# The experts' constants of the second FFN: products on GpSimd in place of most one-column matmuls

## The chip, the cores and the metric

The kernel runs on one core of one Trainium2 chip. The metric is the time of one execution on the device, in microseconds. TensorE multiplies matrices (PE in the rows, PEld its weight loads), VectorE (DVE) and ScalarE (ACT) work on tiles and read TensorE's results, GpSimd (POOL) works on tiles in SBUF alone, and SyncE (SP) issues the transfers.

## The reference, cut to what matters

The network adds four layers to 1024 rows of 256 numbers: an attention and an FFN with two experts, then a second attention and a second FFN with eight experts. The change lies in the second FFN:

```python
for e, (w1, b1, w2, b2) in enumerate(expert_params):
    hm = h * mask[..., e:e + 1]
    acc = acc + (_gelu(_gelu(hm) @ w1 + b1) @ w2 + b2)
out = out + acc * gate[..., k:k + 1]
```

A row that is not the expert's own is masked to zero, and the expert then still gives `_gelu(b1) @ w2 + b2`: a constant vector of 128 numbers for each expert, the same for all rows. The hidden sizes are 128, 256, 384, 512 and the same again, so `w2` of the eight experts has 1, 2, 3, 4, 1, 2, 3 and 4 chunks of 128 rows, 20 in all.

## The kernel before, in words

The rows lie in 8 tiles of 128; the attentions work tile by tile, the FFNs on 4 groups of two tiles. Each layer is cut into small steps, named by layer, tile or group, step and number. `make_orders` is a list scheduler in Python that runs when the program is built: `COST` gives each step's engines and estimated times, `steps_and_needs` what it must wait for, and among the steps that an engine could start next, `URGENCY` (with `SWITCH`, `CHANGE` and `SLACK`) picks one. Each engine then carries out its list strictly in that order, and semaphores see to what it depends on. Tiles of the layers are mixed in this way, so that attention steps fill the waits of the FFN steps.

Steps that the text speaks of:

- First attention, tile t: `ln` writes the normed queries in split form to QS (VectorE); `tq` has SyncE transpose QS into QT by DMA from tile 3 on; `s` scores into a bank S and VectorE's maximum and subtraction (MN, PT); `e` ScalarE's exponential; `p` transposes of PT; `o`, `n` the weighted values and back.
- First FFN, group g: `ln` writes XN; `x` transposes XN into a bank S, and ScalarE copies it to XT; `r` the routing matmuls (WR); `u` a block of up matmuls into a bank H, ScalarE's leaky ReLU to R, GpSimd's square to A; `d` the down matmuls, which read A.
- Second FFN, group 0 only: `b` ScalarE's gelu of the biases, GB1; `z`, four steps of two experts each: 20 fp32 matmuls in all, weights W2 (128x128), moving operand one column of GB1, into banks S, which VectorE negates into Y0n. The last one adds up Cb, which ScalarE reads when it takes the shared expert's result (`y` 0) into ACC; the other experts' results get Y0n as a bias.

In the order before, the four `z` steps stand on TensorE behind the scores of tile 2 and ahead of `x` of the first FFN's group 0. An fp32 matmul shows as two records in the profile. A bank that is to be filled is claimed first: its last reader must be done. All matmuls go through the helper at L1325, so the rows tell them apart by their tiles.

Of the kernel before, what the change touches and what calls it, by code (L numbers as in the profile page):

```python
# [4 lines left out]
fp32 = mybir.dt.float32  # L5
bf16 = mybir.dt.bfloat16
u32 = mybir.dt.uint32
ALU = mybir.AluOpType
ACT = mybir.ActivationFunctionType
AX = mybir.AxisListType  # L10
# [49 lines left out]
def ring_of(s):  # L60

    if (s[0], s[2]) == ("attn0", "s") and s[1] < 2:
# [20 lines left out]
                 e="act .2 dve 1.5", t="act .2 dve 2.0", d="pe .87 act 1.13", g="pe .13 act .36", c="pe .86 act .94",  # L83
                 w="pe .43", y="act .47 dve .88", o="pe 1.3 dve .42", st="sp .5", b="act .22", z="pe 1.12 dve .16")}
COST = {part: {s: [(e, float(d)) for e, d in zip(text.split()[::2], text.split()[1::2])] for s, text in costs.items()}
        for part, costs in COST.items()}
# [8 lines left out]
MODE_CHANGE = 0.09  # L95
SWITCH = 12396.8
CHANGE = 244.4
SLACK = {"act": 0.2, "dve": 0.151, "pe": 0.064, "pool": 0.216, "sp": 0.391}
GELU = {("ffn1", s) for s in "bdc"}
EXP = {("attn0", "e"), ("attn1", "p"), ("ffn0", "g"), ("ffn1", "e"), ("ffn1", "t")}  # L100
URGENCY = {
# [15 lines left out]
}  # L117
# [36 lines left out]
def steps_and_needs():  # L154
# [9 lines left out]
    def need(s, f, part=0, of=-1):  # L164
        needs.setdefault((s, part), []).append((f, of % len(work_of(f))))
# [79 lines left out]
    def ffn1(g):  # L245
        def f(name, i=0, g=g):
            return "ffn1", g, name, i
# [11 lines left out]
        for i, (e, c) in enumerate(WORK):  # L259
            if i % 2 == 0:  # L260
                add(f("c", i // 2), f("d"))
                if i >= 4:
                    need(f("c", i // 2), f("w", min(i + 1, NCH1 - 1) - 4), part=1)
            add(f("w", i), f("c", i // 2))
            if c == CH1[e] - 1 and e == EXPERTS[1]:
                need(f("w", i), f("g"))
            if c == CH1[e] - 1:
                j = EXPERTS.index(e)
                add(f("y", j), f("w", i))
                if j == 0 and g == 0:  # L270
                    need(f("y", j), f("z", E1 // 2 - 1))
        for k in range(2):
            add(f("o", k), f("y", E1))
            add(f("st", k), f("o", k))
        if g == 0:
            add(f("b"))
            for i in range(E1 // 2):
                add(f("z", i), f("b"))
            need(f("t"), ("const", 0, "g", 0))
# [119 lines left out]
def mixed_network(nc: bass.Bass, x, ctx_in, ctxT, wr0, wf0, wp0, wq1, wkv1, wo1, down_w, down_b,  # L399
                  up_w, bias_rows, router_w, router_rows, core_w, w1, b1, w2, b2, out):  # L400
    ctx = ExitStack()
    with ctx:
# [39 lines left out]
        earlier = sb("earlier", [P, E1, E1], fp32)  # L442
        mhalf = sb("mhalf", [P, 2], fp32)
        rbias = sb("rbias", [P, E1], fp32)
        GB1 = sb("GB1", [P, NCH1], fp32)
# [14 lines left out]
        QR = sb("QR", [P, 2, D], fp32)  # L460
        QS = sb("QS", [P, 2, NH0, 64], bf16)
        KR = sb("KR", [P, 2, CTX], fp32)
        KS = sb("KS", [P, 2, NKV0, 4, 64], bf16)
# [180 lines left out]
        biased = sem("biased")  # L644
        zeros_ready = sem("zeros_ready")
        dve_step = sem("dve_step")
        pool_step = sem("pool_step")
# [245 lines left out]
        def _(pool):  # L893
# [61 lines left out]
            def biases(g, _):  # L955
# [5 lines left out]
                for t in (2 * g, 2 * g + 1):  # L961
                    nc.gpsimd.tensor_tensor(X[:, t, :], X[:, t, :], BR[:, 0, :], ALU.add).then_inc(biased, 1)

            def square(g, i):
                n = g * BLOCKS0 + i
# [37 lines left out]
            def gate_rows(*_):  # L1003

                link(nc.gpsimd.memset(flat(selG[:, :, :]), 0.0))
                for part in range(PARTS):
# [9 lines left out]
                         ("ffn0", "v"): norm("ffn0"), ("ffn1", "v"): norm("ffn1"), ("attn1", "kv"): keys1,  # L1016
                         ("ffn1", "i"): biases, ("ffn0", "u"): square})


        @block.vector  # L1020
        def _(dve):
# [235 lines left out]

            def zero_row(g, i):

                b, done = filled(dve, "ffn1", g, "z", i)  # L1260
                nc.vector.tensor_scalar(Y0n[:, 2 * i:2 * i + 2], b[:, 0:2], -1.0, None, ALU.mult).then_inc(done, 1)
                if i == E1 // 2 - 1:

                    total = lsum["ffn1"][:, 0:1]
                    read_out(dve, "ffn1", g, "z", i)
                    dve.wait_ge(ld_small, 16 * SMALL)
                    link(nc.vector.tensor_tensor(Y0s[:, :], B2[:, 0:E1], Y0n[:, :], ALU.subtract))
                    link(nc.vector.tensor_reduce(total, Y0s[:, :], AX.X, ALU.add))
                    nc.vector.scalar_tensor_tensor(Cb[:, :], B2[:, E1:E1 + 1], 0.1, total, ALU.mult, ALU.add
                                                   ).then_inc(zeros_ready, 1)  # L1270

# [33 lines left out]
            def first_queries(t, i):  # L1305
                queries0(t, i)
                if t == 1:
# [9 lines left out]
                 ("ffn1", "v"): variance("ffn1"), ("ffn1", "ln"): rows("ffn1"), ("ffn1", "r"): logits1,  # L1317
                 ("ffn1", "e"): two_largest, ("ffn1", "t"): gates1, ("ffn1", "z"): zero_row,
                 ("ffn1", "y"): expert, ("ffn1", "o"): result_ffn1})
# [3 lines left out]
        def _(pe):  # L1323
# [219 lines left out]

            def zero_row(g, i):
                b, done = claim(pe, "ffn1", g, "z", i)
                if i == 0:
                    pe.wait_ge(ld_w2, 16)
                    pe.wait_ge(gb1_ready, 1)
                for e in (2 * i, 2 * i + 1):
                    for c in range(CH1[e]):  # L1550
                        ch = FIRST1[e] + c
                        ins = mm(b[:, e % 2:e % 2 + 1], W2[:, ch, :], GB1[:, ch:ch + 1], start=(c == 0), stop=(c == CH1[e] - 1))
                ins.then_inc(done, 1)
# [31 lines left out]
            def widen(g, k):  # L1585
# [5 lines left out]
                if k == 0:  # L1591
# [16 lines left out]
                 ("ffn0", "d"): down0, ("ffn1", "x"): turn_rows("ffn1"), ("ffn1", "r"): route("ffn1", XT1, RW, E1),  # L1608
                 ("ffn1", "g"): turn_gates, ("ffn1", "d"): narrow, ("ffn1", "z"): zero_row, ("ffn1", "c"): up1,
                 ("ffn1", "w"): down1, ("ffn1", "o"): widen})  # L1610
# [52 lines left out]
```

## Time and profile before

| | |
|---|---|
| median of 3 runs | 370.07 us (370.01 to 371.87) |
| profiled execution | 374.63 us |
| its span, first to last instruction | 372.8 us |
| TensorE busy | 342.8 us, 92% |
| VectorE, ScalarE, GpSimd busy | 221.9, 179.9 and 96.0 us |
| mean granted clock of TensorE | 0.954 of full speed |

Busy time is read from one execution under the hardware profiler; the median comes from runs of the same program without it. Times in rows count from the span's start.

### The profile page before, as it was taken

The numbers are of one execution on the slowest core, as the hardware profiler recorded it, in microseconds if no ns is written. First come the engines' busy times: TensorE is split into PE (matmuls) and PEld (weight loads), VectorE is DVE, ScalarE is ACT, GpSimd is POOL, SyncE is SP. The second block draws the span as 40 slices with busy tenths as digits, with TensorE's granted clock in tenths as the row PEclk, the third lists the DMA queues.
The fourth block names the chain that finished last, engine by engine and source line by source line (L and its number), as shares of the span: only waits on it lengthen the run. The fifth ranks groups of instructions, "written<-read, shape, count | busy, mean of one in ns | idle before, by whom it ended". The sixth has DMA issues, their size and how long they took to land.

```text
span 372.8 us, 8427 instructions
## 1 busy us (share of the span) xinstructions
PE 342.8 (92%) x3352; PEld 279.6 (75%) x3352; DVE 221.9 (60%) x586; ACT 179.9 (48%) x381; POOL 96.0 (26%) x175
## 2 busy tenths in 40 slices
PE   0677599999999999999999999999999998996996
PEld 0455598887888887878778787888687876784883
DVE  7996976979596825670762265754636483267024
ACT  1656735444542454421222553466586646765462
POOL 7886323332232113134252223310101200020000
PEclk9957958999999999999999999999999999998799
DMA  9999630633603500306300340330042330000000
GB/s 187 417 380 243 133 58 0 114 43 72 114 3 67 102 2 4 58 1 114 57 2 3 35 62 20 59 58 0 22 86 39 58 65 22 2 2 29 0 0 30
DMA packets 62295, 25.75 MB, mean 69 GB/s; under 512 B 58544, under 2 KB 60848, under 8 KB 61488
## 3 DMA queue, kind: packets, MB, share of 16 engines
q1 hardware_dynamic: 62256, 25.21, 30.8%
q8 instruction: 27, 0.44, 0.5%
q14 instruction: 12, 0.10, 0.1%
HBM read 10.52 MB, written 1.05 MB: 31 GB/s over the span
## 4 chain that ended last, share of the span: by engine, by line
PE 81%; DVE 13%; issue 2%; ACT 2%; POOL 1%; DVEq 0%; POOLq 0%
PE Y L1325 27%; PE H L1325 24%; PE S L1325 20%; PE S L1370 5%; PE S L1394 1%; DVE MN L1092 1%; DVE PT L1093 1%; PE S L1403 1%; PE S L1485 1%; DVE K L1079 1%; ACT PT L761 1%; DVE X L1292 1%; DVE K L1302 0%; ACT PT L804 0%; DVE statsf L1041 0%
## 5 line engine op out<-in xcount | busy, mean ns | idle before, releaser
L1325 PE MATMUL H<-XT,WF 128*128 128x256 f32 x256 | 61.5, 388 | 0.0
L1325 PE MATMUL Y<-WP,A 128*128 128x256 f32 x256 | 59.7, 381 | 0.0
L969 POOL TENSOR_TENSOR A<-R 128x512 f32<-128x512 f32 x32 | 33.7, 1056 | 77.2 <-ACT R L837 71.5
L1325 PEld LDWEIGHTS H<-XT,WF 128*128 128x128 f32 x256 | 47.4, 193 | 6.6
L1325 PEld LDWEIGHTS Y<-WP,A 128*128 128x128 f32 x256 | 47.4, 190 | 6.4 <-POOL A L969 0.2
L1325 PE MATMUL Y<-A,W 128*128 128x256 f32 x168 | 46.5, 391 | 0.5 <-DVE KS L1278 0.4
L865 ACT ACTIVATE A<-H,B 128x256 f32<-128x256 f32 x84 | 35.4, 473 | 22.6 <-PE H L1325 22.4
L1325 PE MATMUL H<-CD,W 128*128 128x256 f32 x168 | 44.6, 397 | 0.0
L1278 DVE TENSOR_TENSOR KS<-KS,Y 128x256 f32<-128x256 f32 x32 | 13.4, 420 | 43.2 <-ACT KS L883 42.9
L837 ACT ACTIVATE R<-H 128x512 f32<-128x512 f32 x32 | 19.1, 596 | 37.6 <-PE H L1325 34.2
L1325 PEld LDWEIGHTS H<-CD,W 128*128 128x128 f32 x168 | 32.1, 199 | 5.2
L1325 PEld LDWEIGHTS Y<-A,W 128*128 128x128 f32 x168 | 29.9, 193 | 7.2 <-ACT A L865 1.3
L761 ACT COPY PT<-S 128x512 f32<-128x512 f32 x32 | 18.1, 588 | 21.2 <-PE S L1370 21.2
L804 ACT ACTIVATE PT<-PT 128x512 f32<-128x512 f32 x32 | 19.6, 627 | 9.6 <-DVE PT L1093 9.3
L1370 PE MATMUL S<-identf,PT 128*128 128x128 f32 x128 | 22.1, 320 | 1.0 <-ACT PT L804 1.0
L910 POOL TENSOR_TENSOR rstdf<-varef,mhalf 128x2 f32<-128x2 f32 x8 | 5.6, 700 | 66.1 <-DVE varef L1045 66.0
L761 ACT COPY QT<-S 128x512 f32<-128x512 f32 (+1 forms) x14 | 10.6, 769 | 22.3 <-PE S L1333 13.3
L910 POOL TENSOR_TENSOR rstd<-vare,mhalf 128x1 f32<-128x1 f32 x16 | 9.3, 583 | 45.0 <-DVE vare L1045 45.0
L1092 DVE TENSOR_REDUCE MN<-S 128x8 f32<-128x512 f32 x24 | 16.4, 683 | 7.5 <-PE S L1325 7.5
L1370 PEld LDWEIGHTS S<-identf,PT 128*128 128x128 f32 x128 | 17.9, 168 | 3.9 <-issue 3.1
L883 ACT ACTIVATE KS<-Y,Y0n 128x256 f32<-128x256 f32 x32 | 15.2, 475 | 10.9 <-PE Y L1325 10.4
L1152 DVE CAST KQS<-S 128x768 bf16<-128x768 f32 x8 | 7.7, 958 | 20.2 <-PE S L1325 20.2
(191 smaller groups left out, 590.6 us busy)
## 6 DMA issues: line engine op xcount, KB each, us to landing
W<-in_w SPq DMA_DIRECT2D x2, 1344.0 KB, 11.8
WF<-in_wf SPq DMA_DIRECT2D x2, 1024.0 KB, 7.2
WP<-in_wp SPq DMA_DIRECT2D x2, 1024.0 KB, 9.3
X<-in_x SPq DMA_DIRECT2D x8, 128.0 KB, 7.9
out_dram<-X SPq DMA_DIRECT2D x8, 128.0 KB, 1.7
CD<-in_ctx_in SPq DMA_DIRECT2D x2, 256.0 KB, 5.2
C<-in_ctx_in SPq DMA_DIRECT2D x1, 256.0 KB, 3.0
CT<-in_ctxT SPq DMA_DIRECT2D x1, 256.0 KB, 3.9
```

The costliest lines, as they stand in the source:

```text
L761: nc.scalar.copy(dst(n, i), src(b, i)).then_inc(done, 1)
L804: nc.scalar.activation(e, e, ACT.Exp, scale=HD0 ** -0.5).then_inc(exp_ready, 1)
L837: nc.scalar.activation(R0[:, n % 2, :], b[:, :], ACT.Prelu, alpha=0.5).then_inc(done, 1)
L865: ins = nc.scalar.activation(A1[:, n % 4, :], b[:, k * GT:(k + 1) * GT], ACT.Gelu, bias=B1[:, ch:ch + 1])
L883: nc.scalar.activation(YS[:, j % 2, :], b[:, 0:GT], ACT.Identity, bias=Y0n[:, e:e + 1]).then_inc(ys_ready, 1)
L910: nc.gpsimd.tensor_tensor(dst, src, mhalf[:, 0:dst.shape[1]], ALU.pow).then_inc(rstd_ready, 1)
L969: nc.gpsimd.tensor_tensor(flat(A0[:, n % 2, :, :]), R0[:, n % 2, :], R0[:, n % 2, :], ALU.mult).then_inc(a0_ready, 1)
L1092: link(nc.vector.tensor_reduce(least, scores, AX.X, ALU.max, negate=True))
L1152: link(nc.vector.tensor_copy(s[:, :, 0:3, :], q.unsqueeze(2).to_broadcast([P, NH1, 3, HD1])))
L1278: nc.vector.tensor_tensor(YG[:, j % 2, :], YS[:, j % 2, :], b[:, GT:2 * GT], ALU.mult).then_inc(free["Y", "dve"], 1)
L1325: return nc.tensor.matmul(o, a, b, start=start, stop=stop, skip_group_check=shared)
L1370: ins = nc.tensor.transpose(b[:, i * P:(i + 1) * P], PT[:, t % 2, 4 * c + i, :], identf[:, :])
```

## The change

GpSimd gets a new step, `zp` of group 0. It multiplies each chunk of W2 by its column of GB1, the column broadcast over the 128 outputs (partitions stay the hidden units), and sums an expert's chunks, so that ZS holds one 128x128 tile for each expert: 8 products of 1 to 4 chunks and 10 sums, each chained to the one before. TensorE then sums over the partitions with 8 matmuls (weights ZS, moving operand a column of ones) in one step `z`, and VectorE negates all eight columns at once. ZS and the room for products, ZP, are laid over QS, so the step waits until the queries of the last two tiles have been transposed. The urgencies and the other numbers of the scheduler are new as well, so every engine's order may change.

```diff
-                 w="pe .43", y="act .47 dve .88", o="pe 1.3 dve .42", st="sp .5", b="act .22", z="pe 1.12 dve .16")}
+                 w="pe .43", y="act .47 dve .88", o="pe 1.3 dve .42", st="sp .5", b="act .22", zp="pool 12.0", z="pe 1.8 dve .16")}
...
-            for i in range(E1 // 2):
-                add(f("z", i), f("b"))
+            add(f("zp"), f("b"), ("attn0", TILES - 2, "tq", 0), ("attn0", TILES - 1, "tq", 0))
+            add(f("z"), f("zp"))
...
+        QROOM = QS[:, :, :, :].rearrange("p t h c -> p (t h c)").bitcast(fp32)
+        ZS = QROOM[:, 0:E1 * L].rearrange("p (e l) -> p e l", l=L)
+        ZP = QROOM[:, E1 * L:(E1 + 4) * L].rearrange("p (c l) -> p c l", l=L)
...
+            def zero_products(*_):
+
+                pool.wait_ge(ld_w2, 16)
+                pool.wait_ge(gb1_ready, 1)
+                for t in (TILES - 2, TILES - 1):
+                    turned0(pool, ld_qt, t)
+                for e in range(E1):
+                    n, first = CH1[e], FIRST1[e]
+                    dst = ZS[:, e:e + 1, :] if n == 1 else ZP[:, 0:n, :]
+                    link(nc.gpsimd.tensor_tensor(dst, W2[:, first:first + n, :], GB1[:, first:first + n].unsqueeze(2).to_broadcast(
+                        [P, n, L]), ALU.mult))
+                    if n == 4:
+                        link(nc.gpsimd.tensor_tensor(ZP[:, 0:2, :], ZP[:, 0:2, :], ZP[:, 2:4, :], ALU.add))
+                    if n > 1:
+                        link(nc.gpsimd.tensor_tensor(ZS[:, e, :], ZP[:, 0, :], ZP[:, 1, :], ALU.add))
+                    if n == 3:
+                        link(nc.gpsimd.tensor_tensor(ZS[:, e, :], ZS[:, e, :], ZP[:, 2, :], ALU.add))
+                nc.gpsimd.memset(ones[:, :], 1.0).then_inc(zs_ready, 1)
...
-            def zero_row(g, i):
+            def zero_rows(g, i):
                 b, done = claim(pe, "ffn1", g, "z", i)
-                if i == 0:
-                    pe.wait_ge(ld_w2, 16)
-                    pe.wait_ge(gb1_ready, 1)
-                for e in (2 * i, 2 * i + 1):
-                    for c in range(CH1[e]):
-                        ch = FIRST1[e] + c
-                        ins = mm(b[:, e % 2:e % 2 + 1], W2[:, ch, :], GB1[:, ch:ch + 1], start=(c == 0), stop=(c == CH1[e] - 1))
+                pe.wait_ge(zs_ready, 1)
+                for e in range(E1):
+                    ins = mm(b[:, e:e + 1], ZS[:, e, :], ones[:, :])
                 ins.then_inc(done, 1)
```

Of the scheduler's numbers, those of `u` and of the new step: `"ffn0"` has `u -79511.2 334.9` (before `u -60521.9 18693.8`), `"ffn1"` has `zp 13479.6 -11633`; the first number is what is added to the length of the way to the end, the second is taken off in proportion to the group.

## Rows read from the trace of the kernel before

**Rows 1.** The page: engines, busy us (share of the span) and instructions.
```profile
PE 342.8 (92%) x3352; PEld 279.6 (75%) x3352; DVE 221.9 (60%) x586; ACT 179.9 (48%) x381; POOL 96.0 (26%) x175
```

**Rows 2.** Timeline of TensorE, 30 to 64 us: start, length, line, operation.
```profile
43.61 0.83 PE L1325 MATMUL S<-GB,W 128*128 128x1 f32 x6 [1.69 <-DVE PT L1093]
...
44.93 6.81 PE L1325 MATMUL S<-GB,W 128*128 128x1 f32 x34 [0.49 <-DVE PT L1093]
...
51.60 1.09 PE L1485 MATMUL S<-identf,XN 128*128 128x128 f32 x4
...
54.19 1.71 PE L1325 MATMUL S<-WR,XT 128*128 128x2 f32 x8
...
57.50 2.78 PE L1325 MATMUL H<-XT,WF 128*128 128x256 f32 x8
...
61.22 0.86 PE L1325 MATMUL S<-K,QT 128*64 128x128 bf16 x24
```

**Rows 3.** Timeline of VectorE, 30 to 64 us.
```profile
44.79 0.73 DVE L1051 TENSOR_SCALAR XN<-X,mvf,rstdf 128x256 f32<-128x256 f32 x2
...
50.82 0.42 DVE L1072 TENSOR_TENSOR QS<-QR,QS 128x256 bf16<-128x256 f32 x1
```

**Rows 4.** Windows: length; busy PE, PEld, DVE, ACT, POOL; PEclk, DMA share, GB/s.
```profile
42.00:43.00 1.00, 0.00 (x0) 0.00 (x0) 0.93 (x4) 0.97 (x3) 0.77 (x2) 1.00 0.00 0
...
46.00:47.00 1.00, 1.00 (x6) 1.00 (x6) 0.96 (x4) 0.12 (x1) 0.00 (x0) 0.50 0.00 0
...
59.00:60.00 1.00, 1.00 (x5) 0.73 (x4) 0.42 (x4) 0.00 (x0) 0.00 (x0) 0.86 0.00 0
```

**Rows 5.** Timeline of TensorE, 84 to 136 us.
```profile
101.42 0.95 PE L1325 MATMUL S<-WR,XT 128*128 128x2 f32 x8
...
102.23 0.63 PE L1370 MATMUL S<-identf,PT 128*128 128x128 f32 x4
```

**Rows 6.** Timeline of ScalarE, 30 to 64 us.
```profile
48.27 0.63 ACT L804 ACTIVATE PT<-PT 128x512 f32<-128x512 f32 x1 [0.76 <-DVE PT L1093]
...
52.73 0.58 ACT L761 COPY XT<-S 128x512 f32<-128x512 f32 x1 [3.83 <-PE S L1485]
```

**Rows 7.** Line L717, the transposes of queries: issues, and time to landing.
```profile
L717 SPq DMA_TRANSPOSE QT<-QS x5: 1726/1870/3135, 51.3 to 110.6; - x5
...
DMA to landing us min/median/max: 4.2/4.2/5.9
```

**Rows 8.** Windows, 114.8 to 127.3: tiles S alone (without POOL), then everything.
```profile
114.80:127.30 12.50, 5.22 (x80) 4.35 (x80) 4.82 (x8) 1.56 (x3) 1.00 0.44 82
...
114.80:127.30 12.50, 12.49 (x116) 10.67 (x115) 8.23 (x16) 3.54 (x7) 3.12 (x3) 1.00 0.44 82
```

**Rows 9.** Groups by form on GpSimd: busy us, mean ns of one.
```profile
L969 POOL TENSOR_TENSOR A<-R 128x512 f32<-128x512 f32 x32 | 33.7, 1056 | 77.2 <-ACT R L837 71.5 <-PE Y L1325 5.8
...
L962 POOL TENSOR_TENSOR X<-X,BR 128x256 f32<-128x256 f32 x8 | 5.7, 735 | 6.7 <-DVE XN L1051 6.7
...
L938 POOL TENSOR_TENSOR KS<-KR,KS 128x128 bf16<-128x128 f32 x5 | 2.1, 427 | 0.0
```

**Rows 10.** Timeline of ScalarE, 238 to 252 us.
```profile
244.55 0.47 ACT L876 ACTIVATE KS<-Y,Cb 128x256 f32<-128x256 f32 x1 [0.31 <-PE Y L1325]
```

**Rows 11.** Timeline of GpSimd, 84 to 160 us.
```profile
115.15 1.04 POOL L969 TENSOR_TENSOR A<-R 128x512 f32<-128x512 f32 x1 [0.79 <-ACT R L837]
...
125.09 1.04 POOL L969 TENSOR_TENSOR A<-R 128x512 f32<-128x512 f32 x1 [7.18 <-ACT R L837]
```

**Rows 12.** Timelines of VectorE and, last, GpSimd, 58 to 107 us.
```profile
59.32 0.16 DVE L1206 TENSOR_TENSOR G<-G,pr_ffn 128x4 f32<-128x4 f32 x1
...
105.58 0.89 DVE L1206 TENSOR_TENSOR G<-G,pr_ffn 128x4 f32<-128x4 f32 x1
...
105.40 1.05 POOL L969 TENSOR_TENSOR A<-R 128x512 f32<-128x512 f32 x1
```

**Rows 13.** Windows of 10 us, the end of the kernel.
```profile
340.00:350.00 10.00, 6.75 (x20) 5.29 (x19) 2.96 (x15) 4.78 (x9) 0.00 (x0) 0.66 0.04 14
```

More of the change, by code:

```diff
@@ L95 @@
 MODE_CHANGE = 0.09
-SWITCH = 12396.8
-CHANGE = 244.4
-SLACK = {"act": 0.2, "dve": 0.151, "pe": 0.064, "pool": 0.216, "sp": 0.391}
+SWITCH = 28884.2
+CHANGE = 1197.5
+SLACK = {"act": 0.003, "dve": 0.165, "pe": 0.042, "pool": 0.43, "sp": 0.946}
 GELU = {("ffn1", s) for s in "bdc"}
@@ L270, in ffn1 @@
                 if j == 0 and g == 0:
-                    need(f("y", j), f("z", E1 // 2 - 1))
+                    need(f("y", j), f("z"))
         for k in range(2):
@@ L443, in mixed_network @@
         mhalf = sb("mhalf", [P, 2], fp32)
+        ones = sb("ones", [P, 1], fp32)
         rbias = sb("rbias", [P, E1], fp32)
@@ L645, in mixed_network @@
         zeros_ready = sem("zeros_ready")
+        zs_ready = sem("zs_ready")
         dve_step = sem("dve_step")
@@ L1016, in _ @@
                          ("ffn0", "v"): norm("ffn0"), ("ffn1", "v"): norm("ffn1"), ("attn1", "kv"): keys1,
-                         ("ffn1", "i"): biases, ("ffn0", "u"): square})
+                         ("ffn1", "i"): biases, ("ffn1", "zp"): zero_products, ("ffn0", "u"): square})
         @block.vector
@@ L1256, in gates1 @@
                 nc.vector.tensor_tensor(s[:, :, 2, :], GR[:, :, :], s[:, :, 1, :], ALU.subtract).then_inc(gs_ready, 1)
-            def zero_row(g, i):
+            def zero_rows(g, i):
                 b, done = filled(dve, "ffn1", g, "z", i)
[L1261 to L1270, printed above, removed]
+                nc.vector.tensor_scalar(Y0n[:, :], b[:, 0:E1], -1.0, None, ALU.mult).then_inc(done, 1)
+                total = lsum["ffn1"][:, 0:1]
+                read_out(dve, "ffn1", g, "z", i)
+                dve.wait_ge(ld_small, 16 * SMALL)
+                link(nc.vector.tensor_tensor(Y0s[:, :], B2[:, 0:E1], Y0n[:, :], ALU.subtract))
+                link(nc.vector.tensor_reduce(total, Y0s[:, :], AX.X, ALU.add))
+                nc.vector.scalar_tensor_tensor(Cb[:, :], B2[:, E1:E1 + 1], 0.1, total, ALU.mult, ALU.add
+                                               ).then_inc(zeros_ready, 1)
             def expert(g, j):
@@ L1317, in _ @@
                  ("ffn1", "v"): variance("ffn1"), ("ffn1", "ln"): rows("ffn1"), ("ffn1", "r"): logits1,
-                 ("ffn1", "e"): two_largest, ("ffn1", "t"): gates1, ("ffn1", "z"): zero_row,
+                 ("ffn1", "e"): two_largest, ("ffn1", "t"): gates1, ("ffn1", "z"): zero_rows,
                  ("ffn1", "y"): expert, ("ffn1", "o"): result_ffn1})
@@ L1542, in narrow, with zero_rows @@
                 ins.then_inc(done, 1)
-            def zero_row(g, i):
+            def zero_rows(g, i):
                 b, done = claim(pe, "ffn1", g, "z", i)
-                if i == 0:
-                    pe.wait_ge(ld_w2, 16)
-                    pe.wait_ge(gb1_ready, 1)
-                for e in (2 * i, 2 * i + 1):
-                    for c in range(CH1[e]):
-                        ch = FIRST1[e] + c
-                        ins = mm(b[:, e % 2:e % 2 + 1], W2[:, ch, :], GB1[:, ch:ch + 1], start=(c == 0), stop=(c == CH1[e] - 1))
+                pe.wait_ge(zs_ready, 1)
+                for e in range(E1):
+                    ins = mm(b[:, e:e + 1], ZS[:, e, :], ones[:, :])
                 ins.then_inc(done, 1)
@@ L1608, in _ @@
                  ("ffn0", "d"): down0, ("ffn1", "x"): turn_rows("ffn1"), ("ffn1", "r"): route("ffn1", XT1, RW, E1),
-                 ("ffn1", "g"): turn_gates, ("ffn1", "d"): narrow, ("ffn1", "z"): zero_row, ("ffn1", "c"): up1,
+                 ("ffn1", "g"): turn_gates, ("ffn1", "d"): narrow, ("ffn1", "z"): zero_rows, ("ffn1", "c"): up1,
                  ("ffn1", "w"): down1, ("ffn1", "o"): widen})
```

31 rows, old and new, of the table URGENCY are left out of this document.

## The prediction

> **What bounds the kernel now.** The first view to read is the page's table of engines: TensorE is busy for 342.8 of 372.8 us, so nearly every microsecond taken off TensorE's own queue counts, provided that the work behind it is ready [rows 1]. What the share hides is how that time is spent in the stage that the edit touches. The timeline of TensorE from 43 us on shows it: the constants' matmuls (out S, operands GB and W) are two groups, 6 and 34 records, that is 40 records for 20 matmuls, two for each fp32 one. They run from 43.61 to 51.74 us, and at once behind them come the first transposes of XN, at 51.60 [rows 2]. They are on the chain: VectorE's timeline has XN written at 44.79 + 0.73 = 45.5 us, so the transposes stand ready for 6 us behind the constants [rows 3].
>
> The windows of 1 us show why they last that long: TensorE's granted clock is at its lower level, 1.2 GHz, in every window from 46 to 59 us (0.50), after an idle TensorE from 42 to 43 us, and goes up to 2.4 GHz within the window behind them (0.86), when the wide matmuls of the first FFN (out H, from 57.50) have begun [rows 2, 4]. The 34 records take 6.81 us, 200 ns each. Narrow fp32 matmuls in a stretch at 2.4 GHz (8 records, 128x2) take 102.23 - 101.42 = 0.81 us, 101 ns each [rows 5].
>
> **The change, part by part.** *Removed: 40 one-column records.* Suppose that the other steps stay in the present order. The transposes of XN start at 45.6 instead of 51.60: 6.0 us. Two steps later the routing matmuls (WR) need XT, whose copy follows the fourth exponential in ScalarE's order. That exponential ends at 48.27 + 0.63 = 48.9 and waits on VectorE's scores, not on the constants; so the copy (0.58) ends at 49.5 and the routing starts at 49.6 instead of 54.19, and all behind it, the first wide matmul among it, is 4.6 us earlier (52.9 instead of 57.50) [rows 2, 3, 6]. The next thing that could be late is the transposed queries of tile 3: QS is written at 51.24, a transpose lands 4.2 us after its issue at the least, so 55.4, and their scores, at 61.22 now, would be at 56.6 [rows 2, 3, 7]. That holds. So the gain here is between 4.6 us (this order) and 6.0 us (if the copy of XT is moved ahead of the last exponential). I take 4.6, because it needs nothing of the new order.
>
> *Added on TensorE: 8 matmuls, 16 records.* They come after the last transposes of queries, so inside the stretch at 2.4 GHz: 16 x 0.101 = 1.6 us, on an engine without gaps there [rows 4, 5, 8]. At 1.2 GHz they would take 3.2 us; nothing there speaks for that.
>
> *VectorE and ScalarE.* Four short negations become one; costed at nothing, as VectorE's own waits lie around them. The gelu of the biases keeps its work and its two table loads.
>
> *Added on GpSimd: the products, as one step.* The trace has no such instruction, but its relatives: 1.056 us for 128x512, 0.735 for 128x256, 0.427 for 128x128 [rows 9]. The eight products have 1 to 4 chunks of 128, each size twice: 2 x (0.43 + 0.74 + 0.90 + 1.06) = 6.3 us, the third size taken between its neighbours. The sums: one of 128 (two chunks), two of 128 (three), one of 256 and one of 128 (four): 2 x (0.43 + 0.86 + 1.17) = 4.9. That makes 18 instructions and 11.2 us, and each of them waits for the one before. The planner's table in the diff has 12.0 us for the step; I take 12.5 with the waits, an estimate. It may start when the last transposes of queries have landed: issued at 110.6, so 114.8 us [rows 7].
>
> What covers it? Nothing needs the constants before ScalarE's first read of Cb at 244.55 [rows 10]: they have 117 us to spare (244.55 - 127.3), and the wait itself costs nothing. What counts is what stands behind the step in GpSimd's queue: the squares of the first FFN (A from R), each of which TensorE's down matmuls need. In the present order squares start at 115.15 and at 125.09, with a third between them [rows 11]. The diff's planner gives the step an urgency of 13479.6 against -79511.2 for the squares' step, so it goes first when both are ready: a step from 114.8 to 127.3 would hold three squares, the first by 12 us. TensorE's other work is the cover: in those 12.5 us it spends 5.2 on attention and routing (tiles S) and the rest, 7.3, on up and down matmuls of the first FFN [rows 8]. The up matmuls, taken as half of that, need no square and can go ahead as far as the two buffers of R reach; with them 8.8 us are covered and 3.7 are left. As the step is one entry of 12.0 in the planner's own table, other steps can be put around it, and I cost the block at nothing, with bounds of 0 and 12.5 - 5.2 = 7.3 us.
>
> *GpSimd against VectorE.* One VectorE row shows the price of a busy GpSimd: the same 128x4 multiply takes 0.16 us at 59.32 and 0.89 at 105.58, where it ends at 106.47 together with the square that began at 105.40 and took 1.05 [rows 12]. So some VectorE instructions wait out a whole GpSimd instruction. VectorE is busy for 8.2 of 12.5 us in that window [rows 8], and its 4.3 idle us cover some eight such waits of half a microsecond: nothing is added, and it worsens the second rival if the cover is gone. The Trainium skill (SBUF — State Buffer, section SBUF: two separate sides) states this as an exclusive lock between GpSimd and VectorE instructions with two SBUF inputs, held for the whole instruction; the row agrees. By it 12.5 us of GpSimd could cost VectorE up to that much, by the row's cover nothing.
>
> *The new order.* All urgencies are new, so every queue may be rearranged. What that is worth no row tells. As bounds I take one gap of the kind that TensorE has now, 3.3 us either way (6.75 of 10 us busy from 340 to 350) [rows 13].
>
> *Sum.* -4.6 + 1.6 = -3.0 us. The profiled execution took 374.63 us with a span of 372.8; it becomes 371.6. The median of the runs is 370.07, 4.56 below the profiled one, and so the forecast is **367.1 us**.
>
> **The rivals.** *More is gained.* The whole 6.0 us arrive and the new order closes one gap of 3.3: -6.0 + 1.6 - 3.3 = -7.7, 362.4 us. For it: the gaps exist. Against: nothing in the diff names one.
>
> *The products on GpSimd become the bound (the other sign).* The step holds the squares and TensorE runs out of work: between 3.7 us (the up matmuls go ahead) and 7.3 us (they don't), 5.5 in the middle, gives -3.0 + 5.5 = +2.5, 372.6 us. It decides from a stall of 4.9 us on. For it: the urgencies and the wait of VectorE behind GpSimd. Against: 117 us of room and a planner that knows the length.
>
> *The shift isn't there.* The runs are 4.56 us quicker than the profiled one; if they don't have the low clock, 40 records cost 4.0 us, end near 48.1 us, and the routing, which waits for the exponential until 49.6 anyway, moves hardly. Or the shift is eaten up later by VectorE. Either way only the 1.6 us are left: 371.7 us. Against: the clock falls after an idle stretch that belongs to the kernel, and TensorE has few idle moments later on in which a shift could vanish. The Trainium skill has a rule on this side: in TensorE: Matmul & The Clock Gate, section LDWEIGHTS (loading the stationary operand), a weight load takes its column count divided by 1.2 in ns, 107 for 128 columns, with no word of the clock; by it the 40 loads are an estimated 4.3 us, which is this rival's case. The trace doesn't agree at the low level: 200 ns for each record [rows 2].
>
> **How the numbers follow.** The forecast (364.5 to 369) has 0.45, more gain 0.18, GpSimd as the bound 0.20, no shift 0.17. A measurement of this kernel tells a change from none from 0.5% on, 368.2 and 371.9 us. Faster: 0.40 of the forecast and 0.18, 0.58. Same: 0.05 of the forecast, 0.06 of the GpSimd case (a stall near its lower end) and 0.12 of no shift, 0.23. Slower: 0.14 and 0.05, 0.19. The range runs from 361.5, a little under the second case, to 373.0, a little over the third; 0.07 to 0.1 is left out at either end.
>
> **What the profile will show.** Right, if no one-column matmuls stand before the first transposes of XN and the first wide H matmul starts near 53 us instead of 57.5; if 16 records of ZS against a column of ones take 1.6 us at a granted clock of 1.00; if 18 instructions on GpSimd take 11 to 14 us and TensorE's busy share in that stretch stays at 10 of 10. The forecast is wrong if TensorE has a new gap beside that step that ends on a square, if H starts no earlier, or if the gap at the end of the kernel (340 to 350) grows or goes.

## The result, and the profile after

The changed kernel takes 368.61 us in the median (367.90 to 371.56, 20 runs); the kernel before, run beside it on the same chip, takes 371.90 (369.62 to 374.80, 20 runs). The ratio is 0.9918, with an interval of 0.9890 to 0.9946: 0.8% or 3.05 us faster. The ratios leave out single runs more than 1.5% above the quickest of the same kernel, so a ratio need not be the quotient of the medians beside it. Forecast were -3.0 us and 367.1, with 361.5 to 373.0 as range. The change was met; the absolute time lies 1.5 us above the forecast, which was counted down from a median of 3 runs of before (370.07), where 20 runs have 371.90.

The page of the changed kernel, whose profiled execution took 368.01 us: the span, and the engines with busy us, share and instructions (against [rows 1]).

```profile
span 366.2 us, 8403 instructions
...
PE 334.9 (91%) x3328; PEld 273.2 (75%) x3328; DVE 222.3 (61%) x583; ACT 185.9 (51%) x385; POOL 107.8 (29%) x194
```

TensorE has 24 records and 7.9 us fewer, GpSimd 19 instructions and 11.8 us more. The profiled execution shown of before (374.63 us) is one of its longer ones. A second profile of before, among the experiments, took 369.72 us with a span of 367.9; against that one the changed kernel is only 1.7 us shorter.

TensorE's timeline, 40 to 56 us, the place that the constants have left (against [rows 2]; the helper is now at L1348):

```profile
40.30 0.64 PE L1348 MATMUL S<-K,QT 128*64 128x128 bf16 x16
44.64 1.09 PE L1508 MATMUL S<-identf,XN 128*128 128x128 f32 x4 [3.70 <-DVE XN L1076]
...
46.45 1.84 PE L1348 MATMUL S<-WR,XT 128*128 128x2 f32 x8
48.15 3.51 PE L1348 MATMUL H<-XT,WF 128*128 128x256 f32 x8
51.49 1.47 PE L1393 MATMUL S<-identf,PT 128*128 128x128 f32 x12
52.80 1.89 PE L1348 MATMUL H<-XT,WF 128*128 128x256 f32 x8
```

No one-column matmul is left there; the transposes of XN wait for XN itself, and the first wide block starts at 48.15 us instead of 57.50. The rows also show what the forecast had not reckoned with: the routing (1.84) and the first wide block (3.51; the second one, also eight records, takes 1.89) run slowly. ScalarE's timeline says why they come so early, and the windows say why they are slow (columns as in [rows 4]):

```profile
43.01 0.63 ACT L810 ACTIVATE PT<-PT 128x512 f32<-128x512 f32 x1
45.76 0.59 ACT L767 COPY XT<-S 128x512 f32<-128x512 f32 x1 [2.13 <-PE S L1508]
46.24 0.63 ACT L810 ACTIVATE PT<-PT 128x512 f32<-128x512 f32 x1
```
```profile
41.00:44.00 3.00, 0.00 (x0) 0.00 (x0) 2.79 (x6) 2.60 (x4) 2.67 (x8) 1.00 1.24 251
...
45.00:51.00 6.00, 6.00 (x23) 5.22 (x22) 5.65 (x16) 2.64 (x5) 0.00 (x0) 0.50 0.02 3
...
52.00:60.00 8.00, 8.00 (x90) 6.76 (x89) 5.71 (x16) 4.15 (x10) 5.24 (x11) 1.00 0.21 39
```

The copy of XT now stands ahead of the second exponential, which is the upper case of the forecast's first term. TensorE stands idle from 41 to 44 us, and the granted clock is then 0.50 (1.2 GHz) until 51. Before, the constants ran at that level [rows 2, 4]; now useful work does.

GpSimd's timeline, first and last instructions of the new step (products L979, sums L984, ones L987), and the squares around it (L994):

```profile
121.19 1.04 POOL L994 TENSOR_TENSOR A<-R 128x512 f32<-128x512 f32 x1
122.19 1.14 POOL L979 TENSOR_TENSOR QS<-W,GB 128x128 f32<-128x128 f32 x2
...
132.09 1.04 POOL L979 TENSOR_TENSOR QS<-W,GB 128x512 f32<-128x512 f32 x1
...
134.02 0.46 POOL L984 TENSOR_TENSOR QS<-QS 128x128 f32<-128x128 f32 x1
134.54 0.10 POOL L987 MEMSET ones<- 128x1 f32 x1
134.63 2.04 POOL L994 TENSOR_TENSOR A<-R 128x512 f32<-128x512 f32 x2
```

The step lasts 134.63 - 122.19 = 12.4 us. It begins at 122.19 us and not at 114.8, and two squares stand behind it, not three. TensorE meanwhile, in windows and at the late place of its matmuls:

```profile
120.00:130.00 10.00, 9.43 (x176) 7.48 (x170) 8.04 (x17) 3.36 (x8) 8.61 (x14) 1.00 0.14 26
130.00:140.00 10.00, 9.46 (x270) 8.34 (x265) 1.57 (x5) 5.60 (x13) 6.14 (x10) 1.00 0.02 5
```
```profile
139.59 0.60 PE L1508 MATMUL S<-identf,XN 128*128 128x128 f32 x4
140.03 1.89 PE L1348 MATMUL Y<-WP,A 128*128 128x256 f32 x8
141.76 1.84 PE L1348 MATMUL S<-ones,QS 128*128 128x1 f32 x16
143.46 1.03 PE L1348 MATMUL S<-WR,XT 128*128 128x2 f32 x8
144.35 1.97 PE L1348 MATMUL S<-WO,R 128*128 128x256 f32 x8
```

It idles for 1.1 of 20 us, and the 16 records hold the next step up from 141.76 to 143.46: 1.7 us at a granted clock of 1.00. TensorE's wait near the end (3.25 us at 343.5 in the kernel before) is there again, 3.26 us at 338.3: the gap of [rows 13] neither grew nor went.

### The profile page after: what moved, and what is told of

The parts are those of the page before. It is cut to its first block, busy times and chain, and to the rows that moved or that the text cites. A ratio compares the mean times of both kernels' runs of the same rounds, so it can differ in the third digit from the quotient of the medians.

```text
span 366.2 us, 8403 instructions
## 1 busy us (share of the span) xinstructions
PE 334.9 (91%) x3328; PEld 273.2 (75%) x3328; DVE 222.3 (61%) x583; ACT 185.9 (51%) x385; POOL 107.8 (29%) x194
## 4 chain that ended last, share of the span: by engine, by line
PE 69%; DVE 11%; POOL 7%; issue 6%; ACT 5%; DMA 2%; DVEq 0%; POOLq 0%; ACTq 0%
PE Y L1348 25%; PE H L1348 22%; PE S L1348 15%; PE S L1393 2%; DMA K<-KS 2%; PE S L1417 2%; PE S L1508 1%; ACT A L871 1%; ACT KS L889 1%; PE S L1426 1%; POOL selG L1032 1%; ACT PT L814 1%; DVE K L1104 1%; POOL KQS L958 1%; DVE XN L1076 1%
## 5 line engine op out<-in xcount | busy, mean ns | idle before, releaser
L1348 PE MATMUL H<-XT,WF 128*128 128x256 f32 x256 | 62.9, 393 | 0.0
L1348 PE MATMUL Y<-WP,A 128*128 128x256 f32 x256 | 59.2, 380 | 0.3 <-POOL A L994 0.3
L1348 PEld LDWEIGHTS H<-XT,WF 128*128 128x128 f32 x256 | 47.7, 194 | 8.3 <-issue 1.5
L1348 PEld LDWEIGHTS Y<-WP,A 128*128 128x128 f32 x256 | 47.6, 190 | 6.4 <-POOL A L994 0.4
L994 POOL TENSOR_TENSOR A<-R 128x512 f32<-128x512 f32 x32 | 33.5, 1052 | 58.8 <-ACT R L843 53.6
L1348 PE MATMUL Y<-A,W 128*128 128x256 f32 x168 | 45.0, 387 | 1.0 <-ACT A L871 0.5
L1348 PE MATMUL H<-CD,W 128*128 128x256 f32 x168 | 42.6, 390 | 0.4 <-ACT CD L860 0.4
L1348 PEld LDWEIGHTS H<-CD,W 128*128 128x128 f32 x168 | 32.2, 197 | 5.7 <-issue 0.6
L1348 PEld LDWEIGHTS Y<-A,W 128*128 128x128 f32 x168 | 29.1, 190 | 8.0 <-ACT A L871 2.2
L1393 PE MATMUL S<-identf,PT 128*128 128x128 f32 x128 | 18.9, 290 | 0.7 <-ACT PT L810 0.7
L1348 PE MATMUL S<-PT,V 64*32 64x64 f32 (+1 forms) x768 | 17.0, 238 | 2.6 <-ACT PT L767 1.6
L1348 PEld LDWEIGHTS S<-PT,V 64*32 64x32 f32 (+1 forms) x768 | 13.6, 107 | 6.3 <-issue 3.4
```

What stands on the lines that cost most here:

```text
L994: nc.gpsimd.tensor_tensor(flat(A0[:, n % 2, :, :]), R0[:, n % 2, :], R0[:, n % 2, :], ALU.mult).then_inc(a0_ready, 1)
L1348: return nc.tensor.matmul(o, a, b, start=start, stop=stop, skip_group_check=shared)
L1393: ins = nc.tensor.transpose(b[:, i * P:(i + 1) * P], PT[:, t % 2, 4 * c + i, :], identf[:, :])
```

## The experiments

Each ratio is taken against the kernel before, run on the same chip.

### The changed kernel once more

Nothing is edited.

> The changed kernel itself, timed beside the variants so that they can be compared with it on one chip. All theories: about 368.6 us against about 371.9 of the kernel before, a ratio of 0.99.

Measured: 368.31 us, ratio 0.9897 (0.9850 to 0.9943), span 366.0. The gain repeats.

### The place alone: 20 matmuls put back ahead of the transposes

The new order stays, without products.

```diff
+    orders["pool"] = [s for s in orders["pool"] if s[2] != "zp"]
...
+    orders['pe'].insert(orders['pe'].index(('ffn0', 0, 'x', 0)), ('ffn1', 0, 'z', 0))
...
-                    ins = mm(b[:, e:e + 1], ZS[:, e, :], ones[:, :])
+                    for c in range(CH1[e]):
+                        ch = FIRST1[e] + c
+                        ins = mm(b[:, e:e + 1], W2[:, ch, :], GB1[:, ch:ch + 1], start=(c == 0), stop=(c == CH1[e] - 1))
```

> The order of the changed kernel, but no products on GpSimd: all 20 one-column matmuls as one step of TensorE, ahead of the first transposes of XN, where the kernel before has them. Theory of the place (the gain is that the constants no longer stand ahead of the first FFN in a stretch at 1.2 GHz, less what they cost later): 4.6 to 6 us of shift are lost and 1.7 us of late matmuls saved, so 371.5 to 373 us, no faster than the kernel before. Rival, the new order by itself is the gain: it stays within 1 us of the changed kernel, 367 to 369.6.

Measured: 374.01 us, ratio 1.0043 (1.0007 to 1.0079). TensorE's timeline:

```profile
43.54 8.69 PE L1345 MATMUL S<-GB,W 128*128 128x1 f32 x40 [1.69 <-DVE PT L1115]
52.10 1.09 PE L1505 MATMUL S<-identf,XN 128*128 128x128 f32 x4
...
53.92 1.84 PE L1345 MATMUL S<-WR,XT 128*128 128x2 f32 x8
55.61 2.91 PE L1345 MATMUL H<-XT,WF 128*128 128x256 f32 x6
```

The 40 records are back on the chain at 217 ns each, near their old price (200 ns in [rows 2], 218 in the second profile of before), and the whole gain is gone. The new order alone is worth +0.4%, +1.6 us (0.3 to 2.9 by the interval); moving and shrinking the constants within it is worth 0.9918 - 1.0043 = -1.25% of 372 us, -4.7 us. As the 16 late records cost 1.7 us, the freed place itself gives about 6.4 us. The two traces agree: from the second scores' matmuls (41.22 us here, 40.30 in the changed kernel) to the end of the first eight wide records it is 18.15 us here (to 59.37) and 11.36 there (to 51.66), 6.8 us.

### Moved, not shrunk: 20 matmuls at the late place

The edit to the matmuls as above, at the changed kernel's place; no products. The second kernel does the same in the order of before.

> The order of the changed kernel, but no products on GpSimd: all 20 one-column matmuls where the changed kernel has its 8. Theory of the place, with TensorE as the bound: 40 records instead of 16 at 0.106 us, 2.5 us more than the changed kernel, 371.1. Rival, the products on GpSimd hold TensorE up by as much as they save: the same as the changed kernel, 368.6, or faster.

> The order of the kernel before, with the four steps of constants taken out and all 20 matmuls put as one step ahead of the routing of the first FFN's group 2; no products on GpSimd. Theory of the place: 4.6 us gained early and 40 x 0.106 = 4.2 paid late, so 0.4 under the kernel before, about 371.5, with the first wide matmuls of the first FFN near 53 us. Rival, moving is enough because the early stretch costs more than the trace showed: under 369.5. Rival, the early shift is eaten up by waits later: 374 or more.

Measured: 376.28 us, ratio 1.0064 (1.0020 to 1.0108), and 375.20 us, ratio 1.0062 (1.0030 to 1.0094). The first misses its expectation; of the second's, the rival came true (374 or more). Moving alone is slower than leaving them. TensorE's timeline of the first (its profiled run, 371.65 us, is its quickest), and its windows:

```profile
141.29 4.52 PE L1341 MATMUL S<-GB,W 128*128 128x1 f32 x40
145.67 1.03 PE L1341 MATMUL S<-WR,XT 128*128 128x2 f32 x8
146.56 3.49 PE L1341 MATMUL S<-WO,R 128*128 128x256 f32 x8
```
```profile
145.00:146.00 1.00, 1.00 (x11) 1.00 (x11) 0.08 (x1) 0.00 (x0) 0.00 (x0) 1.00 0.00 0
...
147.00:148.00 1.00, 1.00 (x4) 0.81 (x3) 0.74 (x6) 0.09 (x1) 0.51 (x1) 0.50 0.00 0
```

The 40 records take 4.4 us up to the next step, 2.7 more than the 16. Behind them the granted clock falls to 0.50 although TensorE was busy all the time, and eight records that take 1.97 us in the changed kernel take 3.49: 1.5 us more. Together that is 4.2 us; the span grows by 3.7, as this run is 0.5 us ahead where the step begins. In the order of before the clock is at 0.51 from 150 to 157 us, falling within the 40 records (146.52 to 151.74). In these profiled runs the products on GpSimd save more than 24 records at 101 ns; by the ratios it is 5.4 us. That the number of records makes the difference is not shown: two traces further down have the same fall behind 16.

The second kernel also tests the forecast's first term in the order that it was worked out in. TensorE's timelines of the kernel before and of this one, the scores ahead of the place and, here, the first wide block:

```profile
40.37 1.55 PE L1325 MATMUL S<-K,QT 128*64 128x128 bf16 x32 [0.75 <-ACT QT L761]
```
```profile
38.97 0.75 PE L1343 MATMUL S<-K,QT 128*64 128x128 bf16 x16 [0.75 <-ACT QT L775]
...
51.43 3.37 PE L1343 MATMUL H<-XT,WF 128*128 128x256 f32 x8
```

From the scores to the start of the block it was 57.50 - 40.37 = 17.13 us and is 12.46: 4.7 us less, where 4.6 were forecast. Against the second profile of before (54.80 - 38.33) it is 4.0. The block then takes 3.37 us at the low clock, instead of 2.78 and 1.89, so that its end is 4.1 and 2.5 us earlier.

### Is it their narrowness?

The same kernel with a moving operand of 64 equal columns in place of one.

```diff
-                        ins = mm(b[:, e:e + 1], W2[:, ch, :], GB1[:, ch:ch + 1], start=(c == 0), stop=(c == CH1[e] - 1))
+                        ins = mm(b[:, e * 64:(e + 1) * 64], W2[:, ch, :], GB1[:, ch:ch + 1].to_broadcast([P, 64]), start=(c == 0), stop=(c == CH1[e] - 1))
```

> As the variant of the new order with all 20 matmuls late and no products, but each matmul takes its column of GB1 64 times over: 128x64 in place of 128x1, 40 records as before. Theory of the clock, that the narrowness of the 4.4 us long stretch brings it down to 1.2 GHz for what stands behind: at 64 columns the records take about as long (weight loads set their pace), the clock stays at 2.4 GHz behind them, and the time is 2.5 to 3 us over the changed kernel, 371, against 376.3 with one column. Rival, the clock falls there for another reason, the narrow steps ahead of it: no difference to one column, 375 to 377.

Measured: 371.71 us, ratio 1.0007 (0.9964 to 1.0050). Its profiled run shows 40 records in 4.57 us and the same fall of the clock, with 3.52 us for the eight records behind. So 64 columns don't keep the clock up. The time is the one that the theory forecast, but its mechanism is not there: the number was luck. That its runs are quicker than those with one column is not shown, as the intervals overlap (1.0020 to 1.0108 there).

### Spread instead of shrunk

The 20 matmuls as four steps between wide blocks of the new order, each with VectorE's negation put behind a named step.

```diff
+    orders['pe'].insert(orders['pe'].index(('ffn0', 1, 'd', 5)) + 1, ('ffn1', 0, 'z', 0))
+    orders['dve'].insert(orders['dve'].index(('attn1', 0, 'm', 0)) + 1, ('ffn1', 0, 'z', 0))
...
+    orders['pe'].insert(orders['pe'].index(('ffn0', 1, 'd', 7)) + 1, ('ffn1', 0, 'z', 3))
```

> The order of the changed kernel without products on GpSimd; the 20 one-column matmuls as four steps (6, 14, 6 and 14 records), each behind another block of wide matmuls of the first FFN, about where the changed kernel has its 8. Theory of the clock (in the variant with all 20 in one stretch, 40 records in 4.4 us brought the granted clock down to 1.2 GHz for the wide matmuls behind them, and this is what the late 20 cost beyond their records): no low window near 145 us and only 24 records more than the changed kernel, about 2.5 us, so 371 us, well under the 376.3 of one stretch. Rival, the 20 matmuls cost that much wherever they are: 375 to 377 us.

Measured: 380.16 us, ratio 1.0122 (1.0049 to 1.0195). VectorE's timeline, from a profiled run of 382.62 us, shows that the test spoilt itself:

```profile
127.03 0.16 DVE L1278 TENSOR_SCALAR Y0n<-S 128x2 f32<-128x2 f32 x1 [2.30 <-PE S L1342]
127.10 1.28 DVE L1116 TENSOR_REDUCE MN<-S 128x8 f32<-128x512 f32 x2
```

The first negation waits 2.30 us for TensorE, the maxima behind it come late, and TensorE then idles for 2.6 of the 5 us from 125 to 130. It tells nothing about the fall behind 40 records, but shows what a 0.16 us instruction at a bad place of an in-order queue can hold up.

### The products left out

The changed kernel without the 18 products and sums: a memset of ZS (0.95 us) takes their place, so the constants are zero.

> The changed kernel with the products and sums left out of GpSimd (the room for them is set to zero, so the constants come out as zero); the 8 matmuls and all orders stay. Theory, the products are covered: within 1 us of the changed kernel, 367.5 to 368.5. Rival, the products hold the two squares behind them and TensorE with them: 2 us or more faster than the changed kernel, 366.5 or less.

Measured: 370.60 us, ratio 0.9976 (0.9941 to 1.0011). Leaving them out brings nothing, which fits products that are covered; their cover is measured in the next experiment. Why it came out slower than the changed kernel is open: its profiled run, 375.17 us, is its longest and can't speak for the others. It does show one thing about the clock. Its 16 late records run from 143.90 to 145.60 as in the changed kernel, with TensorE busy 1.00 from 140 us on, and yet the granted clock is 0.50 from 148 to 158 us, where the changed kernel has 1.00.

### The products done twice

```diff
-                for e in range(E1):
+                for e in [*range(E1), *range(E1)]:
```

> The changed kernel with all products and sums on GpSimd done twice, so the step takes 24.6 us in place of 12.4; nothing else is changed. Theory (the step is covered by attention work laid around it, but the cover is about as long as the step): the squares behind it in GpSimd's queue come some 12 us later, the down matmuls with them, and TensorE gets a gap: its third group of XN transposes, at 139.6 us, comes 5 to 10 us later, and the time is 372 to 377 us. Rival (the cover is far longer than the step, because the squares behind it are not needed soon): TensorE stays above 9.4 of 10 us busy from 120 to 150 us and the time stays within 1 us of the changed kernel's, 367.6 to 369.6.

Measured: 382.32 us, ratio 1.0290 (1.0223 to 1.0358). GpSimd's and TensorE's timelines:

```profile
146.82 2.04 POOL L994 TENSOR_TENSOR A<-R 128x512 f32<-128x512 f32 x2
```
```profile
137.54 0.44 PE L1426 MATMUL S<-identf,XA 128*128 128x128 f32 x2
147.91 3.78 PE L1348 MATMUL Y<-WP,A 128*128 128x256 f32 x8 [9.93 <-POOL A L994]
...
152.33 1.06 PE L1508 MATMUL S<-identf,XN 128*128 128x128 f32 x4
```

The squares come 12.2 us later (134.63 in the changed kernel) and TensorE waits 9.93 us for them: the cover is 2.3 us longer than the step, no more. The gap is followed by the low clock (3.78 us for eight down records, 1.89 in the changed kernel), so the third transposes of XN are 12.7 us late; against the changed kernel's ratio it is 13.8 us. The mechanism was the expected one, its size above it because of that second part.

### The change in the order of before

Before's numbers for the scheduler; the products put behind the sixth square of group 1, the 8 matmuls late.

```diff
+    orders['pe'].insert(orders['pe'].index(('ffn0', 2, 'r', 0)), ('ffn1', 0, 'z', 0))
+    orders['pool'].insert(orders['pool'].index(('ffn0', 1, 'u', 5)) + 1, ('ffn1', 0, 'zp', 0))
```

> The order of the kernel before, with the constants' four steps taken out, the products on GpSimd behind the sixth square of the first FFN's group 1, and the 8 matmuls ahead of the routing of group 2. Theory of the place: 4.6 us gained early, 1.7 paid late, no low clock behind the 16 records: 3 us under the kernel before, about 369.5, plus up to 3 for a square that the products hold. Rival, the new order makes the gain: no faster than the kernel before, 372 or more.

Measured: 374.68 us, ratio 1.0059 (1.0020 to 1.0098), slower than before. TensorE's timeline:

```profile
135.78 1.13 PE L1357 MATMUL S<-WO,R 128*128 128x256 f32 x4
140.40 3.68 PE L1357 MATMUL Y<-WP,A 128*128 128x256 f32 x8 [3.49 <-POOL A L1003]
```

GpSimd's step runs from 126.84 to 139.31 and TensorE waits 3.49 us for the square behind it, then runs at a mean granted clock of 0.66 from 140 to 145. The third transposes of XN, at 144.35 us with the 20 matmuls late in this order, are at 150.39, 6.0 us later; 0.6 of these are there already at the matmuls ahead of the wait (135.78 against 135.18), so 5.4 us are lost here. This is the second rival of the forecast, at the place and near the price that it had. The expectation's rival has the number (372 or more), but not the reason that the trace shows. Another place for the products in this order was not tried.

### XN sooner

GpSimd's step for XN's rstdf is put ahead of the keys of tile 5.

```diff
+    orders["pool"].remove(("ffn0", 0, "v", 0))
+    orders['pool'].insert(orders['pool'].index(('attn0', 5, 'c', 0)), ('ffn0', 0, 'v', 0))
```

> The changed kernel with one step of GpSimd moved: the norm of the first FFN's group 0 ahead of the keys of tile 5, which in the profile of the changed kernel waited 2.3 us for a transfer and then took 2.2 us, with the norm behind them. Theory, TensorE's wait for XN (41 to 44.6 us) is on the path: XN is 0.5 to 2 us earlier and the kernel 0.5 to 2 us faster than the changed kernel, 366.5 to 368. Rival, the keys that are now later hold something else: no change or slower.

Measured: 369.84 us, ratio 0.9950 (0.9919 to 0.9982): no gain over the changed kernel. rstdf is ready 1.7 us sooner (begun at 41.63 instead of 43.34), but VectorE begins to write XN at 44.12 all the same (44.08 in the changed kernel), as its queue has two scores' subtractions ahead of it.

TensorE's timeline of this profiled run (375.24 us, its longest), at the 16 late records, belongs to the question of the clock:

```profile
142.23 1.84 PE L1355 MATMUL S<-ones,QS 128*128 128x1 f32 x16
143.93 1.36 PE L1355 MATMUL S<-WR,XT 128*128 128x2 f32 x8
145.15 3.76 PE L1355 MATMUL S<-WO,R 128*128 128x256 f32 x8
```

TensorE is busy 1.00 from 140 to 160 us, and the granted clock is 0.95 from 140 to 145 and 0.50 from 145 to 155: the eight WO records take 3.76 us, as behind the 40 records, where they take 1.97 in the changed kernel. So the fall behind the late constants also comes with 16 records, in two of the seven traces that have them; with 40 at the late place it is in all three. What decides it is open.

### The idle time filled

Sixteen matmuls of the identity with itself, into the bank of the first wide block, while TensorE waits for XN.

```diff
+                    if (part, g) == ("ffn0", 0):
+                        idle, _ = claim(pe, part, g, "u", 0)
+                        for _ in range(16):
+                            mm(idle[:, 0:P], identf[:, :], identf[:, :])
```

> The changed kernel with 16 idle matmuls of the identity by itself (128x128, into a bank that the first wide block overwrites) in TensorE's wait for XN, 41 to 44.6 us. Theory of the clock: the low stretch from 44 to 52 us is the price of that wait; with it filled, the transposes, the routing and the first wide block run at 2.4 GHz, the low window is gone, and the kernel is 2 to 4 us faster than the changed one, 364.5 to 366.5. Rival, the clock falls anyway or TensorE's later waits (scores, exponentials) take the gain: no change, 368 to 369.

Measured: 367.27 us (365.81 to 370.76, 9 runs), ratio 0.9911 (0.9871 to 0.9950). TensorE's timeline:

```profile
42.36 0.64 PE L1348 MATMUL S<-K,QT 128*64 128x128 bf16 x16
42.93 3.84 PE L1348 MATMUL H<-identf 128*128 128x128 f32 x32
46.61 0.60 PE L1512 MATMUL S<-identf,XN 128*128 128x128 f32 x4
...
47.98 1.05 PE L1348 MATMUL S<-WR,XT 128*128 128x2 f32 x8 [0.34 <-DVE PT L1118]
48.89 1.97 PE L1348 MATMUL H<-XT,WF 128*128 128x256 f32 x8
```

The clock stays at 1.00 from 38 to 62 us, as the theory had it. In this execution all of this stage comes 2.06 us later than in the changed kernel's (second scores at 42.36 and 40.30), because TensorE's granted clock was 0.68 from 20 to 40 us, where the other had 1.00. VectorE has XN written at 45.87 + 0.73 = 46.60, so the idle work, which ends at 46.77, does not hold the transposes up. Counted from the scores, the first wide block ends after 8.50 us instead of 11.36: 2.9 us are gained, and 2.4 are still there at 332 us. The late start and a longer low stretch behind 338 us (0.60 to 345 us, 0.76 in the changed kernel) then use up more than that, and the span is 367.1 us against 366.2. The timed runs show no gain: the ratio is that of the changed kernel (0.9918, and 0.9897 when it was repeated), though the quickest run, 365.81 us, is the lowest time of all kernels here. So the price of the idle stretch is shown where it lies; that the kernel gets quicker by it is not.

### A second profile of before

Nothing is edited.

> The kernel before once more, for a second profile of it. If the stretch at 1.2 GHz around the constants belongs to the kernel, it is there again, from 45 or 46 to past 55 us; the one from 18 to 32 us may be there or not, and with it some of the 5 us by which the runs of this kernel differ. Rival of the prediction, the timed runs don't have the low stretch at the constants: then this profile, if its time is near 370, shows 2.4 GHz there.

Measured: 369.72 us, span 367.9. TensorE's timeline:

```profile
43.05 7.42 PE L1325 MATMUL S<-GB,W 128*128 128x1 f32 x34 [0.49 <-DVE PT L1093]
50.33 1.09 PE L1485 MATMUL S<-identf,XN 128*128 128x128 f32 x4
...
54.80 1.89 PE L1325 MATMUL H<-XT,WF 128*128 128x256 f32 x8
```

Here too the constants run at the price of the low clock, 218 ns each, in an execution 4.9 us shorter than the one in [rows 2]. The low stretch is shorter here, though: 0.50 from 44 to 53 us, where it was 46 to 59, so that the first wide block takes 1.89 us and not 2.78. From the scores to the end of that block it is 18.36 us here and 19.91 there, 1.6 of the 4.9 us. More of the difference lies elsewhere: the page's row of granted clock shows low slices at 18 to 37 and 335 to 354 us in the longer run, and less of both in the shorter.

## Why the prediction was right, step by step

**The bound and the place: right.** Putting the 40 records back takes all of the gain away, in the order that the changed kernel has.

**The shift, 4.6 us taken out of 4.6 to 6.0: right for the order of before, too small for the new one.** In the order of before the start of the first wide block moved by 4.7 and 4.0 us against the two profiles. In the new order the freed place gives about 6.4 us, as the copy of XT stands ahead of the later exponentials, the upper case. The first wide block was forecast near 53 us and starts at 48.15; of the 9.35 us one lies ahead of the constants (VectorE's first maximum over the scores there began at 42.13 us and begins at 41.16).

**The late records, 1.6 us: right.** 1.7 us at a granted clock of 1.00. The fall of the clock that can follow them was not foreseen; it is not in the changed kernel's two profiles, but in two others with the same 16 records.

**GpSimd, 12.5 us at no cost: right, by little.** 12.4 us, sizes as worked out from [rows 9], and no gain when they are left out. TensorE's busy share beside it was forecast at 10 of 10 and is 9.4; the 0.6 us gap at 126 us ends on a subtraction of VectorE's (MS), none on a square. The cover is 2.3 us longer than the step. It comes from the order: attention steps were laid around the step, as costed. In the order of before [rows 8, 11] the second rival happens, at +2.2 us (ratio 1.0059) where the forecast had +2.5.

**VectorE behind GpSimd, nothing: nearly right.** Two XN instructions take 1.52 us beside a square and the first products, 1.44 beside a square alone (in the spread kernel), 0.73 at 44.08 beside neither. Beside the products a conversion and a subtraction of MS take 0.47 and 0.35 us, instead of 0.17 and 0.18 in the spread kernel, and TensorE's 0.6 us gap ends on that subtraction. The waits don't add up to the step's length: from 125.8 to 128.5 us the maxima and subtractions that read banks last 0.68 and 0.69 us as ever. The Trainium skill (SBUF — State Buffer, section SBUF: two separate sides) states an exclusive lock between GpSimd and some of VectorE's instructions, held for a whole instruction; the lengthened ones agree with it. No run here shows which instructions take part.

**The new order, nothing: mis-sized.** It costs +1.6 us by itself, within the bounds of 3.3 either way. So the sum is -6.4 + 1.7 + 1.6 = -3.1 us where -4.6 + 1.6 + 0 = -3.0 stood: the total was met with two terms off by 1.8 and 1.6 us that cancel, and that is luck. The 6.4 is worked out from the measured total, so the sum's agreement proves nothing; the traces bear it out with 6.8 and, below, 6.1 us. Nor is the order a cost only: the same change has a ratio of 1.0059 in the old order and 0.9918 in the new one, some 5 us that the change is worth only together with its order. The 5.4 us stall in the old order is the largest part of them that the traces show.

**Where the early microseconds go.** Between the second profile of before and the changed kernel's, the end of the first wide block is 5.0 us earlier (56.69 and 51.66), though the scores ahead begin 1.06 us later (38.33 and 39.39): 6.1 us counted from there. The late records take back 1.7. TensorE idles for 1.1 us between 60 and 140 us where it idled for 0.3, and for 3.7 us instead of 2.4 between 160 and 320. That leaves 1.2 us; the spans differ by 1.7, the rest lies in the end of the kernel. The medians differ by more, 3.3 us, because the runs of before spread further up (to 374.8, against 371.6). The spread goes with the clock: of the 29 runs of before beside the repeat, the six under 370.5 us have mean granted clocks of 0.972 to 0.981, the five above 373.8 us 0.954 to 0.959. What makes the clock differ from run to run was not settled.

**The third rival is out.** It wanted runs without the low clock; the second profile of before, 0.1 us above the lowest of the 20 runs in the result, has it, and the wide block starts earlier in the trace.

## What to carry to other kernels

Work taken out of a place where TensorE runs at its low clock can bring less than its length, since what follows inherits that place (here the first wide block, 1.89 us in the shorter profile of before and 3.51 after): look at what will stand there next. A long step on an engine that others wait for is free only as far as an order has been laid around it, and the same change may lose in the old order. Look at what comes right behind a moved stretch of small matmuls, and in more than one execution: the clock there was not the same in all of them. And line two profiles up at an instruction ahead of the edit before comparing times in them, as their starts can differ by 2 us.

## What the runs showed of the hardware

TensorE's granted clock fell from 1.00 to 0.50 within or behind 40 small fp32 records in a row, with TensorE busy 1.00 in every window, in all three traces that have them at the late place, with 64 columns as with one. Behind 16 such records it fell in two of seven traces; in four of the other five TensorE has the same order. So neither the number of records nor their columns explains it by itself, and the cause is open.

Elsewhere it fell after idle time (41 to 44 us in the changed kernel; 138.0 to 147.9 us with the products doubled). Sixteen useless matmuls in the first of these idle stretches kept it at 1.00, and the eight wide records behind took 1.97 us instead of 3.51.
